# A relation-aware graph layer on one core: the edge index work moved into the K/V projection, more queries gathered ahead, and the layer norm's small steps shared by four node tiles

## The reference

```python
Q = (einsum('nc,rch->rnh', x, Wq) + bq[:, None, :]).reshape(5, 6250, 4, 64)   # K and V likewise
q_i, k_j, v_j = Q[edge_type, dst], K[edge_type, src], V[edge_type, src]
score = sum(q_i * k_j, axis=-1) / 8
seg = dst * 5 + edge_type                       # softmax over the edges of one node and relation
e = exp(score - segment_max(score, seg)[seg])
alpha = e / segment_sum(e, seg)[seg]
out = segment_sum(v_j * alpha[..., None], dst, num_segments=6250).reshape(6250, 256) + bias
y = x + out
return (y - mean(y)) / sqrt(var(y) + 1e-5)      # over the 256 channels
```

## Time and profile before

| | us |
|---|---|
| median of 3 runs | 2538.89 |
| lowest and highest | 2535.01 and 2538.93 |
| the profiled execution's own time | 2540.96 |
| its span in the trace | 2539.1 |

### The profile page before, as it was taken

One profiled execution on the slowest core, in us unless ns is written; L12 is line 12 of the kernel. 1 busy time (PEld: TensorE's weight loads), 2 busy tenths in 40 slices (PEclk: granted clock), 3 DMA queues, 4 the chain that ended last, 5 costly groups with the idle time before them and its releaser, 6 DMA issues.

```text
span 2539.1 us, 26489 instructions
## 1 busy us (share of the span) xinstructions
PE 1619.8 (64%) x5873; PEld 1124.9 (44%) x5873; DVE 1729.1 (68%) x3784; ACT 1205.2 (47%) x4119; POOL 1633.8 (64%) x1745
## 2 busy tenths in 40 slices
PE   6999999999990355555455555554555455555547
PEld 2444544444440344444444444444444444444445
DVE  8888544444445777777777777777777777777658
ACT  2232210000001666666666666666666666666656
POOL 1000657777777777777777777777777777777404
PEclk9999999999995566666666565666666665566675
DMA  6333789999999766666666666666666666666305
GB/s 197 112 123 114 260 295 362 363 364 360 363 359 328 222 200 201 201 200 200 199 200 202 200 201 201 199 200 201 202 202 200 202 201 200 200 200 200 107 9 178
DMA packets 286449, 553.97 MB, mean 218 GB/s; under 512 B 43789, under 2 KB 168543, under 8 KB 286290
## 3 DMA queue, kind: packets, MB, share of 16 engines
q0 software_dynamic: 106496, 327.26, 43.3%
q1 hardware_dynamic: 143556, 157.07, 18.6%
q10 hardware_dynamic: 36238, 67.94, 7.6%
HBM read 398.44 MB, written 153.65 MB: 217 GB/s over the span
## 4 chain that ended last, share of the span: by engine, by line
POOL 33%; PE 26%; issue 16%; ACT 9%; DVE 9%; DMA 6%; SPq 0%; DVEq 0%; ACTq 0%; POOLq 0%
POOL region L398 22%; PE sums L557 20%; POOL region L403 10%; ACT region L791 8%; DVE region L873 5%; DMA region<-q_tab,qidx 4%; PE sums L618 3%; DMA q_pre<-region 1%; ACT pairs L780 1%; PE sums L554 1%; DVE region L1156 1%; DVE region L1159 1%; DMA region<-in_x 0%; DVE acc L1078 0%; DVE acc L1145 0%
## 5 line engine op out<-in xcount | busy, mean ns | idle before, releaser
L618 PE MATMUL sums<-region 128*128 128x130 f32 x3328 | 777.6, 417 | 775.6 <-ACT region L791 744.2
L618 PEld LDWEIGHTS sums<-region 128*128 128x128 f32 x3328 | 707.7, 318 | 833.6 <-ACT region L791 828.5
L398 POOL DMA_INDIRECT region<-kv_tab,kvidx x832 | 794.7, 955 | 255.3 <-issue 245.4
L791 ACT ACTIVATE region<-region 128x64 f32<-128x64 f32 x3328 | 822.2, 335 | 0.0
L557 PE MATMUL sums<-region,acc 128*128 128x512 f32 (+2 forms) x1568 | 673.0, 577 | 0.9 <-DVE region L995 0.9
L379 POOL DMA_INDIRECT region<-q_tab,qidx x391 | 373.1, 954 | 386.7 <-DMA q_tab<-region 258.3
L780 ACT COPY pairs<-region 128x1024 f32<-128x1024 f32 x208 | 211.3, 1016 | 772.2 <-DMA region<-q_pre 449.7
L1078 DVE TENSOR_TENSOR acc<-acc,sums 128x256 f32 x832 | 348.9, 419 | 289.2 <-PE sums L618 215.4
L403 POOL DMA_INDIRECT region<-q_tab,qidx x441 | 420.2, 953 | 134.5 <-issue 132.3
L557 PEld LDWEIGHTS sums<-region,acc 128*128 128x128 f32 (+1 forms) x1568 | 286.7, 190 | 309.8 <-issue 299.7
L995 DVE TENSOR_TENSOR region<-sums,region 128x512 f32<-128x512 f32 (+1 forms) x245 | 169.1, 691 | 245.7 <-PE sums L557 242.5
(11 more groups left out here) (188 smaller groups left out, 835.5 us busy)
## 6 DMA issues: line engine op xcount, KB each, us to landing
kv_tab<-region ACTq DMA_DIRECT2D x48, 1280.0 KB, 7.8
q_pre<-region SPq DMA_DIRECT2D x391, 128.0 KB, 5.2
region<-q_pre SPq DMA_DIRECT2D x391, 128.0 KB, 3.5
q_tab<-region SPq DMA_DIRECT2D x48, 640.0 KB, 3.2
region<-q_tab,qidx POOLq DMA_INDIRECT x832, 3.9
region<-kv_tab,kvidx POOLq DMA_INDIRECT x832, 3.6
region<-in_x SPq DMA_DIRECT2D x96, 128.0 KB, 3.1
out<-region SPq DMA_DIRECT2D x48, 128.0 KB, 1.9
```

The lines of the kernel that those rows point to most:

```text
L398: pool.indirect_dma_start(ring[:, s % KS, i, :], None, kv_tab, bass.IndirectOffsetOnAxis(ap=kvidx[:, t:t + 1], axis=0)).then_inc(s_got[s % ...
L618: done = nc.tensor.matmul(bank[i][:, h * W:(h + 1) * W], ring[:, q % KS, i, h * P:(h + 1) * P], oneh[:, q % 2, i, :], start=True, stop=True)
L791: done = nc.scalar.activation(ring[:, q % KS, i, h * D:(h + 1) * D], ring[:, q % KS, i, C + h * D:C + (h + 1) * D], ACT.Copy, scale=alT[:, ...
```

## The change

Four things are edited.

1. Z goes from OS - 4 = 107 to NOQ - 3 = 144, and in DVE's loop `indices(o - Z)` runs only for `o >= Z + 4`. Steps 4 to 14 thus run after chunks 148 to 158, `cast_rows` and `shift_rows` after chunks 149 and 152, the 26 `turn_same` after chunks 157 to 182, steps 41 and 42 after chunks 185 and 186. K and V begin with chunk 147. OS and OA stay.
2. `AHEAD` after the first 12 steps goes by (2, 2, 1, 2, 2) instead of (2, 2, 1, 2). Counted out, `PRE` gets 48 + 2 x 196 - 40 = 400 entries instead of 48 + 2 x 196 - 49 = 391 (the words given with the change say 401).
3. In the norm, square root, reciprocal and shift are done for four node tiles in one instruction each (13 groups, the last of one tile); `ys` and `of` get eight places instead of four.
4. SP's loop in the norm loads tile u + 8 and stores tile u - 4 in its round u, instead of tile u.

```diff
-    AHEAD = [SB if s < 12 else (2, 2, 1, 2)[s % 4] for s in range(NSB)]
+    AHEAD = [SB if s < 12 else (2, 2, 1, 2, 2)[s % 5] for s in range(NSB)]
...
-    Z = OS - 4
-    assert OA < NOQ and Z + 15 + NCK + 4 < NO, Z
+
+    Z = NOQ - 3
+    assert OS < OA < NOQ and Z + 15 + NCK + 4 < NO, Z
...
+        def group(g):
+
+            assert NT % 4 == 1
+            k = min(4, NT - 4 * g)
+            return (P if 4 * g + k < NT else LASTN), 4 * (g % 2), k
...
-            for t in range(NT):
-                if t + XQ < NT:
-                    sp.wait_ge(s_y, t + 1)
-                    load_xf(t + XQ)
-                sp.wait_ge(s_o, t + 1)
...
+            for u in range(NT + 4):
+                if u + XQ < NT:
+                    sp.wait_ge(s_y, u + 1)
+                    load_xf(u + XQ)
+                t = u - 4
+                if t >= 0:
+                    sp.wait_ge(s_o, t + 1)
+                    for lo, hi in parts(t):
+                        sp.dma_start(out[t * P + lo:t * P + hi, :], of[lo:hi, t % 8, :]).then_inc(s_of[t % 8], 16)
...
-                act.wait_ge(s_norm, t + 1)
-                if t >= 4:
-                    act.wait_ge(s_of[t % 4], 16 * (t // 4))
...
+                act.wait_ge(s_norm, t // 4 + 1)
+                if t >= 8:
+                    act.wait_ge(s_of[t % 8], 16 * (t // 8))
...
-            for t in range(NT):
-                n = nodes(t)
-                act.wait_ge(s_var, t + 1)
-                nc.scalar.activation(std[0:n, t % 2:t % 2 + 1], mv[0:n, t % 2, 1:2], ACT.Sqrt, bias=eps_t[0:n, :]
+            for g in range((NT + 3) // 4):
+                n, lo, k = group(g)
+                act.wait_ge(s_var, 4 * g + k)
+                nc.scalar.activation(std[0:n, lo:lo + k], mv[0:n, lo:lo + k, 1], ACT.Sqrt, bias=eps_t[0:n, :]
                                      ).then_inc(s_std, 1)
-                if t > 0:
-                    normalize(t - 1)
-            normalize(NT - 1)
+                for t in range(4 * g, 4 * g + k):
+                    normalize(t)
...
-                indices(o - Z)
+                if o >= Z + 4:
+                    indices(o - Z)
...
+            def scale(g):
+
+                n, lo, k = group(g)
+                dve.wait_ge(s_var, 4 * g + k)
+                dve.wait_ge(s_std, g + 1)
+                c(nc.vector.reciprocal(rstd[0:n, lo:lo + k], std[0:n, lo:lo + k]))
+                nc.vector.scalar_tensor_tensor(out=shift[0:n, lo:lo + k], in0=mv[0:n, lo:lo + k, 0], scalar=-1.0,
+                                               in1=rstd[0:n, lo:lo + k], op0=ALU.mult, op1=ALU.mult).then_inc(s_norm, 1)
+
+            for t in range(NT):
+                moments(t)
+                if t >= 4 and t % 4 == 0:
+                    scale(t // 4 - 1)
+            scale((NT - 1) // 4)
```

More of the change, by code:

```diff
@@ L222, in gnn_kernel @@
         bias_sb = cut(C)
-        of = cut(4 * C).rearrange("p (s c) -> p s c", s=4)
-        ys = cut(4 * C).rearrange("p (s c) -> p s c", s=4)
+        of = cut(8 * C).rearrange("p (s c) -> p s c", s=8)
+        ys = cut(8 * C).rearrange("p (s c) -> p s c", s=8)
         M4, D4, w4, dw4, rd4, wn4, mg4, d4 = cut(H), cut(H), cut(H), cut(H), cut(H), cut(H), cut(H), cut(H)
@@ L230, in gnn_kernel @@
         stats = cut(2 * 6).rearrange("p (s n) -> p s n", s=2)
-        mv = cut(2 * 2).rearrange("p (s n) -> p s n", s=2)
-        std, rstd, shift = cut(2), cut(4), cut(4)
+        mv = cut(8 * 2).rearrange("p (s n) -> p s n", s=8)
+        std, rstd, shift = cut(8), cut(8), cut(8)
         sums = ctx.enter_context(nc.psum_tensor("sums", [P, 4, 512], f32))
@@ L277, in gnn_kernel @@
         s_xb, s_yp = sem("s_xb"), sem("s_yp")
-        s_of = [sem(f"s_of{i}") for i in range(4)]
+        s_of = [sem(f"s_of{i}") for i in range(8)]
         s_y, s_var, s_std, s_norm, s_o = sem("s_y"), sem("s_var"), sem("s_std"), sem("s_norm"), sem("s_o")
@@ L475, in _ @@
                 load_xf(t)
-            for t in range(NT):
-                if t + XQ < NT:
-                    sp.wait_ge(s_y, t + 1)
-                    load_xf(t + XQ)
-                sp.wait_ge(s_o, t + 1)
[L481 to L484, removed]
+            for u in range(NT + 4):
[7 more added lines that the diff above has]
+                        sp.dma_start(out[t * P + lo:t * P + hi, :], of[lo:hi, t % 8, :]).then_inc(s_of[t % 8], 16)
+            for i in range(8):
+                sp.wait_ge(s_of[i], 16 * (len(range(i, NT, 8)) + (1 if (NT - 1) % 8 == i else 0)))
         @block.tensor
@@ L1152, in moments @@
                 dve.wait_ge(s_xb, t + 1)
-                if t >= 4:
-                    dve.wait_ge(s_o, t - 3)
-                nc.vector.tensor_tensor(ys[0:n, t % 4, :], bank[t % 4][0:n, 0:C], xf[0:n, t % XQ, :], ALU.add
+                if t >= 8:
+                    dve.wait_ge(s_o, t - 7)
+                nc.vector.tensor_tensor(ys[0:n, t % 8, :], bank[t % 4][0:n, 0:C], xf[0:n, t % XQ, :], ALU.add
                                         ).then_inc(s_y, 1)
                 dve.wait_ge(s_y, t + 1)
[L1159 to L1174, removed]
-                if t > 0:
-                    scale(t - 1)
+                c(nc.vector.bn_stats(stats[0:n, t % 2, :], ys[0:n, t % 8, :]))
+                nc.vector.bn_aggr(mv[0:n, t % 8, :], stats[0:n, t % 2, :]).then_inc(s_var, 1)
+            def scale(g):
[10 more added lines that the diff above has]
+            scale((NT - 1) // 4)
 _INS = ["x", "src", "dst", "edge_type_5", "L0_gnn_Wq", "L0_gnn_bq", "L0_gnn_Wk", "L0_gnn_bk", "L0_gnn_Wv",
```

4 lines of the change are left out of this document (2 added, 2 removed).

## The result

The changed kernel takes 2521.4 us (median of 4 runs, 2516.02 to 2522.28), the kernel before 2538.91 in the same comparison (4 runs, 2535.01 to 2540.34): ratio 0.9928 [0.9916, 0.9939], faster by 0.7%. The forecast was 2514, range 2507 to 2525: the time lies in the range, but above the own range of 2509 to 2519. The two profiled executions lie 2539.1 - 2514.2 = 24.9 us apart in span, which is the predicted sum of 24.8. That agreement flatters it. The profiled execution of before took 2540.96 us, more than any timed run of it, and the one of after 2516.02, the fastest of its runs. The medians are only 17.5 us apart.

A forecast was written before the change was run, and what follows sets the result against it. POOL's unbroken gathers were taken as the bound from 343.27 to 2376.36 us, and DVE in the norm. Savings of 3.5 (main loop's start), 11.3 (nine gathers) and 10.0 (norm) sum to 24.8 us: 2538.89 to 2514, range 2507 to 2525.

The forecast's parts named there:

- own range: Whole kernel: the forecast's narrower range, 2509 to 2519 us, before it was widened to 2507 to 2525.
- Q part: Q stage: without the moved index work it ends 17.4 us earlier; POOL's 49th gather at 325.9, wrong if over 332.
- stalls for the index handshakes: K/V stage: PE waits on DVE and evictions around the moved index work, 1.5 us taken, bounds 0 and 3.4.
- the lock step of PE and ACT (2553): Rival, K/V stage: 26 `turn_same` hand-overs each lose 1.5 us, 39 us in all, making it slower, 2553; chance 0.02.
- The index steps and the gathers: K/V stage: moved DVE operations stretch two of POOL's gathers, 1.7 us, bound 4.2, at no cost to the total.
- the rival's price 10: Rival, gathers ahead: ten DVE index operations each block a gather about 1 us, POOL free at 777, 2520; chance 0.08.
- together 3.5 us: Main loop's start: begins at 771, 2 us earlier, and the 1.90 us stop before the fourth step goes; bounds 0 and 7.
- the sign that the 11.3 are wrong: Main loop: POOL showing waits for ACT there would disprove the 11.3 us gain from nine gathers fewer.
- Nine gathers: Main loop: nine gathers move ahead of it, 1264 instead of 1273, 9 x 1.26 = 11.3 us less while POOL bounds.
- Norm: Norm: 1.10 us a tile, 12.5 us less, but 2.5 more at the end; net 10.0, bounds 6 and 12.5.
- The rival of a tile at 1.3 us: Rival, norm: something other than DVE, likely x loads, holds a tile at 1.3 us, so no gain, 2526.6; chance 0.07.
- Theory C: Whole kernel, stated with the experiments: the sum is right and the difference to the medians is one slow profiled execution.

The follow-up runs named there:

- before_again: The kernel before, unedited, run again for a second profile; 2531.41 us, ratio 0.9995 against before at 2532.6.
- changed_again: The changed kernel, unedited, run again on another chip; 2512.24 us, ratio 0.9917 against before at 2532.93.
- ahead_only_2: Kernel before with only 400 instead of 391 tiles gathered ahead, index work and norm as before, usual data speed; 2533.37 us, ratio 1.0002 against before.
- all_two: Changed kernel with two queries' tiles ahead in every step from the 12th on, 440 instead of 400; 2513.03 us, ratio 0.9914 against before.
- z_only_2: Kernel before with only the index work moved, 391 tiles ahead, old norm, usual data speed; 2527.99 us, ratio 0.998 against before.
- no_stop: Changed kernel with FIRST = 7 instead of 3 and no POOL wait for the query ring in steps gathering no queries; 2510.07 us, ratio 0.991 against before.
- z_ahead_2: Kernel before with index work moved and 400 tiles ahead, old norm, usual data speed; 2522.11 us, ratio 0.9957 against before.
- z_only: Kernel before with only the index work moved, in the slow-data series; 2955.24 us, ratio 0.9969 against before at 2963.82.
- z_ahead: Kernel before with index work moved and 400 tiles ahead, old norm, in the slow-data series; 2940.15 us, ratio 0.9918 against before.

## Why the prediction held, and what was off

A fairer pair for the sum is `before_again` and `changed_again` (2528.7 - 2511.7 = 17.0 us of span, by medians 19.2), though from two chips, whose medians of the kernel before are 2532.6 and 2532.93; the pair predicted on gives 24.9. Term by term:

```
term                         predicted   before/after   before_again/changed_again
fourth step earlier          3.5         1.1            -0.1
fourth step to last gather   11.3        14.3           8.9
last gather to norm          0           -0.4           -0.7
norm                         12.5        12.0           11.1
end                          -2.5        -2.2           -2.2
```

- **Q part.** 17.4 us earlier was predicted; the last Q chunk's evictions end at 321.4 (322 predicted) and the 49th gather is at 328.19, 2.3 later than the 325.9 forecast, under the 332 that would have refuted it. What was missed is that the faster Q stage runs into its stores: DVE's last evictions wait for them, and the 49th gather comes 6.8 us behind the last eviction, 3.9 before. In the traces of the kernel before, no eviction waits for them. This fence is DVE in the changed kernel, in order of time:

```profile
319.81 1.62 DVE L997 TENSOR_TENSOR region<-sums,region 106x512 f32<-106x512 f32 x3 [1.56 <-DMA q_tab<-region]
322.34 0.69 DVE L1003 TENSOR_TENSOR region<-sums,region 128x512 f32<-128x512 f32 x1 [0.92 <-PE sums L566]
```

  Over the stage these waits are 13.6 us in 5; PE waits 0.2 us for an eviction in all.
- **K/V stage.** The stalls for the index handshakes were bounded by 3.4 us, 1.5 taken. PE in order of time shows one before `shift_rows` and one before the first `turn_same`; a third of 0.81, for an eviction, is at 415.52. Sum 1.96, under the 4 that would have refuted it:

```profile
333.47 1.13 PE L534 MATMUL pairs<-region 128*128 128x512 f32 x2 [0.29 <-DVE recS L938]
...
345.97 0.33 PE L543 MATMUL pairs<-ident,region 128*128 128x128 f32 x1 [0.86 <-ACT region L721]
...
346.38 1.98 PE L566 MATMUL sums<-region,acc 128*128 128x512 f32 x4
...
348.56 1.98 PE L566 MATMUL sums<-region,acc 128*128 128x512 f32 x4
```

  From one `turn_same` to the next PE takes 348.56 - 346.38 = 2.18 us, the 2.17 that it took in the Q part: the lock step of PE and ACT (2553) isn't there. The last K/V eviction ends at 761.6 (763 forecast, 761.35 before).
- **The index steps and the gathers.** Behind the 49th gather five are longer than 1 us: the four of the fence above and one of 1.07 at 342.44. They lose 0.49 + 0.44 + 0.22 + 0.83 + 0.12 = 2.1 us against 0.95; the prediction took 1.7, its bound was 4.2, the rival's price 10. It had the size about right and read the mechanism wrong ("the stretching, not its full size"). This fence is DVE under the four gathers of the first fence of POOL, at 334.45, 346.32, 349.26 and 351.99:

```profile
334.05 1.01 DVE L944 TENSOR_TENSOR region<-region,recS 128x832 f32<-128x832 f32 x1
...
345.88 1.01 DVE L963 TENSOR_TENSOR region<-region 128x832 f32<-128x832 f32 x1
...
348.59 1.02 DVE L967 SCALAR_TENSOR_TENSOR nrel<-region 128x832 f32<-128x832 f32 x1
...
351.93 1.02 DVE L974 SCALAR_TENSOR_TENSOR nrel<-region,nrel 128x832 f32<-128x832 f32 x1
```

  Each of these gathers began while the operation ran and ends 0.82 us after it: 346.32 + 1.39 = 347.71 against 345.88 + 1.01 = 346.89, and 351.99 + 1.78 = 353.77 against 351.93 + 1.02 = 352.95. The same holds in all fourteen traces for the 73 gathers that begin inside a DVE operation of this length, unless it ends within 0.15 us anyway. A gather that is already under way isn't touched: the one at 350.73 keeps its 0.95 across L972's start at 350.87. So a held gather is held to the operation's end, and the ten operations cost 2.1 us and not 10 because only five gathers began inside one with more than 0.15 us of it left, and were held for the rest alone. The Trainium skill ("SBUF — State Buffer", section "SBUF: two separate sides") says that on the shared ports the one that comes second fully blocks; the trace agrees for the gathers, but shows no DVE operation held by a gather: L948 began at 338.96, 0.27 us into a gather, and took 1.02 us like the others. POOL was free at 770.0 instead of 768.6, as the 49th gather was 2.3 us later.
- **The main loop's start: the mis-sized term.** The step that failed is "together 3.5 us". It had two halves: a start at 771 instead of 772.99, and the stop of 1.90 us that "goes". The start came at 770.78, after a wait of 0.77 for `kv_tab` (1 to 5 forecast). But at the fourth step POOL waited 2.98 us for the query copies, more than before: they can run only after `s_ready`, which came at 779.8, 10.7 us after the last gather ahead (774.6 and 8.9 predicted). The prediction had named waits of POOL for ACT in the main loop as the sign that the 11.3 are wrong; this is the only one longer than the 0.3 us that lies between any two gathers, and it belongs to the first term instead. ACT in order of time, its first copy for the main loop:

```profile
786.70 1.02 ACT L789 COPY pairs<-region 128x1024 f32<-128x1024 f32 x1 [385.61 <-DMA region<-q_pre]
```

  It ends at 787.72, and the fourth step starts 0.7 behind it. (The 1.64 us before the next gather, at 791.05, are no wait for a copy: the profile names no releaser. `changed_again` has 1.34 there and `ahead_only_2` 1.64, before and `before_again` 0.3; the cause is not shown.) So the fourth step is the later of two things, start + 15.0 and the first copy's end + 0.7. Start + 15.0 went from 788.0 to 785.8 in the first pair and from 785.4 to 787.0 in the second, the copy's end from 788.9 to 787.7 and from 786.1 to 785.9; the later of the two gained 1.1 and -0.1 us. The first half was measured from a slow row as well. In `before_again` the main loop starts at 770.40, with no wait for `kv_tab`; in the six kernels with early index steps (`all_two` aside) it starts at 768.2 to 772.0, with one. K and V are ready no sooner, as PE's work only changed places (the last K/V eviction started at 760.66 before and at 760.88 after), and when they land differs by 4 us from one execution to the next. Where they landed earliest, in `z_only_2` and `no_stop`, the fourth step gained what was predicted, 3.5 and 3.6 us against `before_again`, in `no_stop` only because its edit had removed the wait for the copy.
- **Nine gathers.** 9 x 1.26 = 11.3 was predicted; the pairs give 14.3 and 8.9. The count effect is the same in both; what differs is the pace over some 1260 gathers: 1.2593 us in before, 1.2544 in `before_again`, 1.2570 in after, 1.2563 in `changed_again`. 0.005 us of pace is 6 us of the total. Between before and `before_again` nearly all of it, 5.8 us, is the length of the gathers themselves (954.4 against 949.8 ns on the mean of 1273, 66 against 42 of them over 1 us) and not a wait. A sum priced to the tenth from one execution can't be better than that.
- **Norm.** 1.10 a tile and 54.0 us predicted, 1.10 and 54.5 measured; the end 4.0 us predicted against 1.43, a loss of 2.5, and 2.2 found (5.9 against 3.7 from the last moments to the end of the span). That PE would not take over was worked out for its lower level; this fence is one stretch at each level in the changed kernel's norm, in the columns of the earlier trace rows:

```profile
2470.00:2472.00 2.00, 1.36 (x9) 0.98 (x9) 1.86 (x7) 0.69 (x2) 1.30 (x2) 1.00 0.78 233
...
2492.00:2494.00 2.00, 2.00 (x9) 1.85 (x8) 1.90 (x6) 0.97 (x3) 1.31 (x3) 0.50 0.71 202
```

  At the lower level PE looks full, 2.00 of 2, and DVE keeps its pace: from L1165 at 2490.51 to the one four tiles on at 2494.92 it takes 4.41 us, at the full clock from 2468.23 to 2472.73 it takes 4.50. PE's busy share was not the limit, as the prediction had read from the earlier trace rows. The rival of a tile at 1.3 us is refuted.
- **Sum and median.** Applied to the median, 24.8 us was 4 to 7 too many: the timed gain is 17.5 us in the first comparison and 20.7 in `changed_again`'s. By `z_ahead_2` 10.5 of it are the first two parts (14.8 predicted), and by the traces 8.9 the norm (10.0 predicted); 19.4 together lies between the two. Theory C holds in part: the profile of before was of its slowest execution, with a 49th gather 1.6 us later and a norm 1.1 us longer than in `before_again`. With the fourth step of `before_again`, 786.9 instead of 789.6, the first term is 0.9 instead of 3.5, and with its norm the third is 1.1 smaller: a sum of 21. That the two profiled spans differ by just the sum is luck: in that pair the pace gave 3.0 more than the 11.3, and the first term 2.4 less than the 3.5. What made that execution slow is shown only so far as its longer gathers.
- **Not tried.** The norm alone at the usual level was not run. Nothing tested the bound under `kv_tab` itself, by making K and V's last stores smaller or earlier.

## What to carry to other kernels

Where one engine issues work without a gap through two stages, moving work over their border is worth at most the hole there: find the hole (here 10.93 us, opened by the first edit, of which the medians gave back 5.9 and the profiled spans 10.2), fill it, and expect nothing of more. Before a sum is taken from one profiled execution, compare that execution's time with the median, and set the uncertainty of a pace times its count (0.005 us x 1260) beside the terms. When small operations per tile are joined into groups, price the end of the stage too: here 2.2 of 11 to 12 us went back.

## What the runs showed of the hardware

The unchanged kernel before took 2963.82 us (median of 16 runs) in one series and 2532.6 (27 runs) in a later one on a chip of the same number, with spreads of under 0.6% within each. POOL's issue of a gather took 0.95 us in both. What differed was the data: 293 against 360 GB/s between 500 and 550 us (`z_only` against `z_only_2`), the first K/V gather at 923.51 against 768.36, and a main loop at 1.47 instead of 1.256 us a gather. At that level nine gathers fewer took 1853.7 - 1831.2 = 22.5 us out of the main loop (`z_only` against `z_ahead`), 2.5 each, twice their issue; that this is their data's time is argued from the GB/s and not shown. A ratio from such a series stands for another bound. Only the norm kept its lengths, and in it the data was not slower: 176 GB/s in `z_only`, 174 in `z_only_2`. Why the data was slow isn't shown.

PE's granted clock over the norm was 0.55 in all five traces with the old norm of the usual level (before, `before_again`, `z_only_2`, `ahead_only_2`, `z_ahead_2`) and 0.84 to 0.94 in the five with the new one, for the same matmuls in 66 and 55 us. In the new norm the clock didn't set the length, as the two stretches above show (4.41 and 4.50 us for four tiles at 0.50 and at 1.00). Why the clock came out higher is not shown.

A gather whose issue begins while DVE runs an operation of 128 x 832 float32 (1.01 to 1.02 us) is held to that operation's end and ends 0.82 us after it; one begun before the operation keeps its 0.95 us, and the operation its length.
